# A grouped attention's last step in a kernel of eight blocks: output products on undivided sums, weights split a step sooner, the ranking's closing passes on GpSimd, and a re-ordered tail

## What is computed

```python
# L2 cross attention: 32 query heads, 8 key/value groups, head size 128
q, kk, v = x @ Wq.T, ctx @ Wk.T, ctx @ Wv.T       # q and kk with an RMS norm per head
out = softmax(q @ kk.T * 128 ** -0.5 + mask) @ v @ Wo.T
# L2 ffn: router of 64 experts, the best 8, their bias rows mixed by weight
# L3 cross attention: for each position the 154 largest of 256 channels of ctx are "crucial"
mask = zeros.at[top_k(ctx, 154).indices].set(1.0)
out = mask * x * A1 + (1 - mask) * x * A2          # A1, A2 from a conv1d and a batch norm
# L3 ffn: a dense product, and the best 2 of 8 low-rank pairs
out = x @ Wb.T + bias + 2 * einsum(h, w, Bm)
```

## Time and profile before

| | us |
|---|---|
| runs: median (lowest to highest of 3) | 875.66 (873.38 to 875.95) |
| the profiled execution, its own time | 870.15 |
| its span, first to last instruction | 868.4 |
| PE busy in the span | 779.3 (90%) |
| DVE busy | 712.1 (82%) |
| ACT busy | 519.6 (60%) |
| POOL busy | 429.5 (49%) |
| granted TensorE clock, mean share of full speed | 0.968 |

### The profile page before, as it was taken

How to read it: one execution, slowest core, us unless ns; L and a number is a source line. 1 busy time by engine, 2 the same in 40 slices (tenths; PEclk the granted TensorE clock), 3 DMA queues, 4 the chain that set the end, 5 groups by cost and what they waited for, 6 DMA issues and landing times. The chain is left out here.

```text
span 868.4 us, 16410 instructions
## 1 busy us (share of the span) xinstructions
PE 779.3 (90%) x5124; PEld 631.2 (73%) x5124; DVE 712.1 (82%) x1756; ACT 519.6 (60%) x1408; POOL 429.5 (49%) x380
## 2 busy tenths in 40 slices
PE   1976899958987999999999999999999999578878
PEld 0474676634676898998898898898898898465446
DVE  7878998968787887887887887887887887974874
ACT  6865798836466756756656656657557557321520
POOL 3237078705135745745745746745745845722110
PEclk9999999979999999999999999999999999889879
DMA  8254246553201201201301300300310310203001
GB/s 316 83 169 148 75 148 214 159 170 104 63 36 55 92 26 52 94 24 44 101 24 33 112 24 24 118 27 21 106 43 9 105 56 1 72 25 118 1 0 49
DMA packets 39115, 68.24 MB, mean 79 GB/s; under 512 B 5729, under 2 KB 18593, under 8 KB 38946
## 3 DMA queue, kind: packets, MB, share of 16 engines
q1 hardware_dynamic: 39074, 67.73, 23.5%
HBM read 62.38 MB, written 5.34 MB: 78 GB/s over the span
## 5 line engine op out<-in xcount | busy, mean ns | idle before, releaser
L1966 ACT ACTIVATE layer_attention_probs<-xnT,stats 128x512 f32<-128x512 f32 x128 | 93.9, 733 | 134.4 <-DVE stats L2075 134.4
L2244 DVE TENSOR_SCALAR_CACHE_REDUCE xn<-ctxT,candidate 128x512 bf16<-128x512 f32 x240 | 168.8, 741 | 0.0
L1750 PE MATMUL bank<-layer_attention_keysT,layer_attention_queriesT 128*128 128x512 f32 x384 | 122.2, 426 | 5.0 <-DVE layer_attention_queriesT L2068 5.0
L2087 DVE TENSOR_TENSOR layer_attention_probsT<-bank,layer_attention_probsT 128x512 fp32r<-128x512 f32 x128 | 88.1, 688 | 39.8 <-ACT layer_attention_probsT L1974 38.3
L1750 PEld LDWEIGHTS bank<-layer_attention_probsT,layer_attention_values 128*128 128x128 f32 x768 | 98.8, 189 | 19.2 <-issue 9.1
L1750 PE MATMUL bank<-layer_attention_probsT,layer_attention_values 128*128 128x256 f32 x768 | 102.3, 282 | 10.2 <-DVE layer_attention_probsT L2087 10.1
L1750 PE MATMUL bank<-layer_attention_wo,layer_attention_headsT 128*128 128x512 f32 x384 | 102.1, 409 | 3.9 <-issue 3.1
L1974 ACT CAST layer_attention_probsT<-bank 128x512 fp32r<-128x512 f32 x128 | 74.8, 584 | 50.8 <-PE bank L1826 50.8
L1696 POOL TENSOR_TENSOR layer_attention_mixed<-layer_attention_mixed,xnT 128x512 f32<-128x512 f32 x32 | 52.5, 1641 | 86.0 <-DMA xnT<-inverse_sums 84.5
L1750 PE MATMUL bank<-layer_attention_l_wq,layer_attention_xnT 128*128 128x512 f32 x384 | 93.6, 392 | 0.0
L1750 PEld LDWEIGHTS bank<-layer_attention_l_wkv,layer_context_parts 128*128 128x128 f32 x720 | 88.5, 188 | 2.7
(11 more groups left out here) (322 smaller groups left out, 1662.9 us busy)
## 6 DMA issues: line engine op xcount, KB each, us to landing
layer_attention_l_raw_qo<-in_wqT SPq DMA_DIRECT2D x9, 1024.0 KB, 5.0
xnT<-inverse_sums SPq DMA_DIRECT2D x16, 512.0 KB, 3.7
layer_attention_l_raw_qo<-in_woT SPq DMA_DIRECT2D x8, 1024.0 KB, 6.9
tw_raw<-in_w_gateT SPq DMA_DIRECT2D x8, 688.0 KB, 5.5
...
```

Source lines behind the costliest of these rows:

```text
L1750: last = pe.matmul(out, stationary[f][a], moving[f][b], start=f == 0 and x == 0, stop=f == count - 1 and x == 2)
L1966: a.activation(probs[:, u % 3, :], masked[:, u % 2, :], ACT.Exp, bias=negmax[:, u:u + 1], scale=-1.0, accum_out=sums[:, u:u + 1]).then_inc ...
L2087: v.tensor_tensor(probsT[:, 1, p % 2, :, columns], T[u % 2][:, :].rearrange("p (c q) -> p c q", c=CPB), probsT[:, 0, p % 2, :, columns], A ...
L2244: own(k.nc.vector.tensor_scalar((k.flags if flags is None else flags)[:, r % 2], row_tile(k.ctxT, r), k.candidate[:, r:r + 1].bitcast(F32) ...
```

## The change

In `layer2_attention`:

- **Step 15 has its own code on every engine (`run_last`).** The mixed heads are split straight out of bank `V`, undivided, into a part of `xnT2` that is free by then (`last_high`, `last_low`). The output products are made per head and tile into five banks (`project_last`). VectorE multiplies each result by the reciprocal of its unit and adds it to `x` in one pass (`add_last`).
- **Weights.** The loads and splits of the ninth group go, and its copy in the inputs. The last group's output weights are loaded in its place and split in step 14, into the query weights' buffer.
- **Choice.** Pieces 3 and 4 become GpSimd's `finish_choice`: two comparisons, a product and a sum per pair, after step 14's heads. Step 14 holds pieces (0,0), (0,1), (2,0), (0,2); step 15 the others, at the units shown.
- **Products spread.** Step 15's output products for step 14 stand at units 4, 6 and 7 instead of 5, 6 and 7, the first mix at unit 3 instead of 2.

In `tail`: the router's products stand between the transposes; 22 filler products instead of 10 ahead of the third set of transposes; and the closing product in three split parts, with one more cast on ScalarE and subtraction on VectorE for each operand.

```diff
-    CHOICE = {STEPS - 2: (0,), STEPS - 1: (2, 4, 6)}
+    CHOICE = {4: (0, 0), 5: (0, 1), 6: (2, 0), 7: (0, 2)}
+        wo_last = wq
+        LAST = (R, J[0], J[1], S[0], S[1])
+        last_heads = lambda part, h: xnT2[:, part, h, 0:SEQ]
...
@@ GpSimd
+                def finish_choice(r):
+                    both = k.ctxT[:, r // B, :].rearrange("p (j c) -> p j c", j=2)
+                    ranks, equal = both[:, :, 0:SEQ], both[:, :, SEQ:2 * SEQ]
+                    g.wait_ge(S_["bisection"], OWN_RANKED[r])
+                    for j in range(2):
+                        g.tensor_scalar(ranks[:, j], ranks[:, j], k.left[:, r + j:r + j + 1], None, ALU.is_le)\
+                         .then_inc(S_["choice_kept"], 1)
...
+                    g.tensor_tensor(equal, ranks, equal, ALU.mult).then_inc(S_["choice_kept"], 1)
...
+                    g.tensor_tensor(ranks, choice_flags[r][:, :, 0:SEQ], equal, ALU.add).then_inc(S_["choice_made"], 1)
...
-                run((None, STEPS - 1), last=True)
+                run((None, STEPS - 3))
+                run((None, STEPS - 2), more=False)
                 for j in range(2):
-                    scale_heads((None, STEPS - 1), j)
+                    o_weights_low(final, j)
+                for j in range(2):
+                    scale_heads((None, STEPS - 2), j)
+                for r in (0, 2, 4, 6):
+                    finish_choice(r)
...
@@ TensorE
+                def project_last(h, t):
+                    i = TPB * h + t
...
+                    if i >= len(LAST):
+                        pe.wait_ge(S_["last_added"], i - len(LAST) + 1)
...
+                    product(LAST[i % len(LAST)][:, :], [[last_heads(a, h)[:, t * P:(t + 1) * P] for a in range(2)]],
+                            [[wo_last[:, x, h, :] for x in range(2)]]).then_inc(S_["last_psum"], 1)
...
@@ ScalarE
+                def last_high(p):
+                    a.wait_ge(S_["mix_psum"], at(final, PAIRS, p + 1))
+                    a.copy(last_heads(0, p), V[:, 0:SEQ]).then_inc(S_["last_high"], 1)
...
@@ VectorE
+                def last_low(p):
+                    v.wait_ge(S_["last_high"], p + 1)
+                    v.tensor_tensor(last_heads(1, p), V[:, 0:SEQ], last_heads(0, p), ALU.subtract).then_inc(S_["last_low"], 1)
...
+                    v.scalar_tensor_tensor(k.x[:, tile, :], LAST[i % len(LAST)][:, :], inverse[:, i:i + 1], k.x[:, tile, :],
+                                           ALU.mult, ALU.add).then_inc(S_["last_added"], 1)
...
@@ tail, TensorE
-                for t in range(TILES):
-                    expert_logits(t)
+                    expert_logits(t - 1)
+                expert_logits(TILES - 1)
...
-                keep_busy(3, 10)
+                keep_busy(3, 22)
...
-                    pe.matmul(last_bank(t)[:, :], lowT[:, t * P:(t + 1) * P], bm[:, :],
-                              start=False, stop=True, skip_group_check=True).then_inc(S_["out_psum"], 1)
+                    for i, (a, b) in enumerate(PARTS):
+                        last = pe.matmul(last_bank(t)[:, :], lowT[:, a, t * P:(t + 1) * P], bm_parts[:, b, :],
+                                         start=False, stop=i == len(PARTS) - 1, skip_group_check=True)
```

334 lines of the change are left out of this document (220 added, 114 removed).

## The result

The changed kernel takes 857.60 us, the median of 4 runs (857.38 to 862.75), against 874.52 for the kernel before on the same chip (4 runs, 871.13 to 875.95). The ratio is 0.9848, 95% interval 0.9814 to 0.9883. Six more runs of it later on gave 858.84 beside 871.36, ratio 0.9847 (0.9819 to 0.9876). By these ratios the gain is 13.3 us, with an interval of 10.2 to 16.3 in the first set of runs and 10.8 to 15.8 in the second. The plain differences of the medians are 16.9 and 12.5; the first rests on four runs a side and is the less reliable. The profiled execution took 857.56 with a span of 855.9, 12.5 less in span than the one before.

What follows compares the result with a forecast made beforehand. TensorE was taken to bound the attention up to 740 us, VectorE the last step, with GpSimd's wait at its end. Closing chain -4.3, body -6.6 and tail -2.1 gave -13.0: median 862.7 from 875.66, range 857 to 869.5.

Steps and rivals of the forecast that it cites:

- rival 1: Last step: only cycle counts, TensorE's lists slip into neighbouring units; body -11.5, median 857.1; chance 12%.
- Steps 13 and 14: Dropped loads and splits for a group that doesn't exist are worth nothing, since TensorE has no idle time there.
- Closing chain: Last step's end, last low-part pass to last sum: no scaling through memory, no GpSimd; 8.9 instead of 13.2, -4.3 us.
- Start at 743.2: Last step's first low-part pass, after two scans that wait 2.0, a sum of 0.69 and a short wait.
- Units: Last step's eight units: 2.7 us each at VectorE's cycle, TensorE setting 4.2 in unit 4 and 4.3 in unit 6; 25.2.
- Finishing: GpSimd's end of the choice: two comparisons at 0.5, a product and a sum; 3.1 us a pair, 12.4 in all.
- Rival 2: Last step: GpSimd's passes hold VectorE's; body gains only 0.7 to 3, median 867.3, at worst 869; chance 22%.
- Rival 3: TensorE held at 1.2 GHz through units 4 to 7: 11 us more, 873.7, no change; chance 4%.
- rivals 4 and 5: 4: GpSimd comparisons dear, median some 1,330, chance 2%. 5: end chain still gated by something unseen, 871.7, chance 3%.
- Tail: After the attention: interleave -0.5, twelve more fillers -1.1, closing products -0.5; -2.1 in all.
- interleave: Tail's entry: two or three of the router's four product tiles fill waits for the rows; -0.5.
- The rest: Tail behind the router's sum: 1.6 us less forecast, fillers -1.1 and closing products -0.5.

Runs made afterwards that it cites:

- tail_only: The kernel before with the tail of the changed kernel; 869.15 us, ratio 0.9989 to the kernel before.
- scans_earlier: The changed kernel with two step 14 pieces exchanged: pair 0's scans in unit 6, pair 2's comparison passes in unit 7; 856.32 us, ratio 0.9818.
- no_finish: The changed kernel with GpSimd's finishing of the choice left out, so not computed; 857.43 us, ratio 0.9842.
- fillers_in_step: scans_earlier with filler products added in the attention's last step, ahead of units 2 and 3's transposes and behind TensorE's last product; 857.52 us, ratio 0.9835.
- attention_only: The changed kernel with the tail of the kernel before; 862.14 us, ratio 0.9903 to the kernel before.
- after_again: The changed kernel, unchanged, run again in a later set; 858.84 us, ratio 0.9847 to the kernel before.
- choice_on_vector: The changed kernel with the choice's comparison and last sum put back on VectorE; 862.43 us, ratio 0.9905.
- equality_summed: scans_earlier with the equality passes also writing a running sum that nobody reads; 858.41 us, ratio 0.9844.
- earlier_no_finish: scans_earlier with GpSimd's finishing of the choice left out; 854.28 us, ratio 0.9801.
- scans_earlier_again: scans_earlier run a second time as a yardstick; 856.23 us, ratio 0.9829.
- ten_fillers: The changed kernel with 10 instead of 22 filler products ahead of the tail's last transposes; 861.19 us, ratio 0.9867.

## Why the prediction was right, and where it was off

The forecast was -13.0; the ratios give -13.3 and the spans -12.5. The measured median itself, 857.60, is 5.1 under the forecast's 862.7 and beside rival 1's 857.1, but that is mostly scatter of the base, 875.66 from three runs, where the later sets of runs of the kernel before have medians of 869.88 to 872.71. The profiled execution came at 857.56 for 857.2, and the stretches are the forecast's own case, not rival 1 (units 24.63 for 25.2, not 21.6) or 2. The total agrees better than its parts. The attention gave 11.5 from zero to the tail for 10.9, the tail 1.1 for 2.1, and these two misses cancel in part. No run takes the closing chain's part out by itself; it rests on the rows of before and after, where GpSimd's wait of 19.9 us and its passes behind it are gone. By its steps:

- *Steps 13 and 14 at nothing.* Step 14 took 32.71 in both (zero less the same event of step 13), which agrees, though four other executions with the new attention had 33.99 to 34.11. That zero moved by only 0.09 is luck: after was 1.34 earlier at that event of step 12 and lost 1.43 in step 13 (34.56 for 33.13). The loss isn't the change's: all executions but the one of before took 34.41 to 34.70 there, tail_only with its old attention too. The forecast had read "no idle time" from rows of step 14 alone; between 673 and 677, in step 13, TensorE is busy for 3.86 of 4 us before, 2.40 after and 3.27 in tail_only.
- *Closing chain, -4.3.* Measured -4.54: a chain of 8.62 for 8.9. The copy took 0.37 for 0.4, the subtraction 0.42 for 0.45, the additions 5.35 for 5.5. The half-size estimates and the overlap of 0.67 held.
- *Start at 743.2.* It was 743.53. The term was mis-sized, and by luck a second error hid it. I let the scans wait 2.0, like the pass of before; they waited 3.3 (4.59), two scans against two halves of a split and then the scaling. What made up for it in part was that the sum and the low-part pass came directly behind. That wait was the largest single loss that these runs found, and one exchange of two pieces took it away: scans_earlier.
- *Units, 25.2.* Measured 24.63. Units 0 to 3 and 5 took 14.03 for 14.0, unit 4 4.37 for 4.2, unit 6 4.10 for 4.3, unit 7 2.13 for 2.7. The sum was right but not all of its reasons. 0.8 of unit 3's 3.45 and 1.0 of unit 4's 4.37 were held passes, as no_finish showed, and in unit 4 I had named TensorE's products alone.
- *Finishing, 3.1 a pair.* It took 4.3 to 4.6. This is the term that was mis-sized most. A comparison of 256 columns cost 0.92, not 0.5. The row that I chose (a select of 64 columns in 0.56) was a poor measure for it. Still the last pair ended at 775.4, before the last addition, so nothing hung on it. The rule of the Trainium skill (GPSIMD Engine Reference, 3.1 Elementwise) is about data-dependent branching, and I had put a comparison under it, 2.6 by estimate. The profile shows about a third of that, so this comparison isn't a case of the rule; on the rule itself no run here tells. Its price was also overdrawn: a last pair from 771.5 on with 7.2 ends 1.4 behind my sum's end of 777.3, not 2 to 3.
- *Rival 2 (GpSimd holds VectorE).* Its mechanism is real: 3.3 at the start and 1.7 in the units, and its sign, a held pass above 1.5, came once, in the two scans of 4.59. It was mostly inside the forecast's terms. *Rival 3* showed in unit 0 at most (a granted clock of 0.57 from 744 to 748); *rivals 4 and 5* had nothing for them (comparisons of 0.92, a chain of 8.62).
- *Tail, -2.1.* The profile gives -1.1 and it is the entry that failed: -0.5 was forecast, +1.21 measured, the interleave's 0.4 to 0.5 less 1.6 for fillers at the half clock. The rest gave 2.3 for 1.6. With the entry at the full clock the new tail takes 76.4 to 76.7 (tail_only, no_finish, scans_earlier, fillers_in_step), which is 2.9 to 3.2 under the 79.57 of before, and 1.6 to 1.9 under the 78.30 of the old tail in attention_only. So of the 2.3 in the rest some 1.3 may be chance: the old tail's first dense product took 4.15 before and 3.37 in attention_only. I had priced the interleave and not asked what TensorE does before it: its last product of the attention now ends 1.4 us before VectorE's last addition, and no term of the sum had that wait.

Ten profiled executions had some 2 us or more (1.97 to 2.84) without work ahead of these fillers. Six found the half clock there (after, after_again, choice_on_vector, equality_summed, earlier_no_finish, scans_earlier_again), four the full one (attention_only, no_finish, scans_earlier, ten_fillers). The four with 1.32 or less (before, tail_only and the two with added fillers) all had the full one. That fits a wait that brings the fall within reach without deciding it, but four profiles don't show it, and no time here does. What decides between the six and the four is open.
